# Four-layer AdaLN kernel on one core: modulation by rows, input in three pieces, a masked triangle, a 64-row last tile, and a new order in the last feed-forward's slot

## What is computed

```
mod = (silu(c) @ wmod).reshape(16, 6, 1, 256)     # per layer: sa, ca, ga, sb, cb, gb
ga  = (2*(ga >= 0) - 1) * max(|ga|, 0.25)          # gb the same
h = layernorm(x) * (1 + ca) + sa ; x = x + ga * attention(h)
h = layernorm(x) * (1 + cb) + sb ; x = x + gb * feed_forward(h)
```

## Time and profile before

| | us |
|---|---|
| median of three runs | 2000.65 |
| lowest, highest | 1992.62, 2005.60 |
| profiled execution, own time | 1990.36 |
| its span (first to last instruction) | 1987.9 |
| TensorE busy in the span | 1742.5 |
| VectorE busy | 1369.3 |
| GpSimd busy | 936.9 |
| ScalarE busy | 758.7 |

### The profile page before, as it was taken

How to read it: one execution, slowest core, us unless ns; L and a number is a source line. 1 busy time by engine, 2 the same in 40 slices (tenths; PEclk the granted TensorE clock), 3 DMA queues, 4 the chain that set the end, 5 groups by cost and what they waited for, 6 DMA issues and landing times.

```text
span 1987.9 us, 41551 instructions
## 1 busy us (share of the span) xinstructions
PE 1742.5 (88%) x14264; PEld 1252.0 (63%) x14264; DVE 1369.3 (69%) x3592; ACT 758.7 (38%) x1530; POOL 936.9 (47%) x984
## 2 busy tenths in 40 slices
PE   8999999689997999999999878889867788998776
PEld 5666665589994555555555556666656566886443
DVE  5788888365554566666666658888746776886765
ACT  3555554122221656565656531111122213443332
POOL 1467666575554446464545353223243223664333
PEclk7999998799997999999999989999998888999887
DMA  6100000100006564545455300000001000000111
GB/s 219 49 18 11 16 16 7 33 10 11 8 14 116 130 118 83 117 88 114 90 110 94 69 13 11 8 8 8 22 26 41 15 15 14 17 13 14 40 34 48
DMA packets 70565, 93.86 MB, mean 47 GB/s; under 512 B 10408, under 2 KB 64792, under 8 KB 67224
## 3 DMA queue, kind: packets, MB, share of 16 engines
q1 hardware_dynamic: 70440, 92.15, 20.6%
HBM read 61.84 MB, written 29.49 MB: 46 GB/s over the span
## 4 chain that ended last, share of the span: by engine, by line
PE 59%; DVE 19%; issue 8%; POOL 7%; ACT 5%; DMA 1%; DVEq 1%; SPq 0%; ACTq 0%; POOLq 0%
PE PS L1101 17%; PE PS L2093 4%; POOL l_ms L1063 3%; DVE negmax L2421 3%; PE PS L2183 3%; PE PS L2057 3%; PE PS L1268 3%; PE PS L529 2%; ACT pw L2336 2%; PE PS L2118 2%; PE PS L2077 2%; DVE xn L519 1%; PE PS L1813 1%; PE PS L2196 1%; PE PS L790 1%
## 5 line engine op out<-in xcount | busy, mean ns | idle before, releaser
L2421 DVE TENSOR_REDUCE negmax<-PS 128x2 f32<-128x512 f32 (+1 forms) x384 | 246.9, 685 | 167.6 <-PE PS L2093 161.7
L560 POOL TENSOR_TENSOR X<-X,y_sb 128x512 f32 (+1 forms) x128 | 164.1, 1282 | 121.7 <-DVE y_sb L555 116.7
L539 ACT ACTIVATE hT<-PS,modT 128x256 f32<-128x256 f32 x256 | 130.5, 562 | 139.8 <-PE PS L529 138.2
L1101 PE MATMUL PS<-we_hi,h_parts 128*128 128x512 f32 x512 | 177.6, 407 | 1.7 <-POOL h_parts L1550 1.5
L555 DVE TENSOR_TENSOR y_sb<-PS,ga_sb 128x512 f32<-128x512 f32 x96 | 66.2, 689 | 156.8 <-PE PS L1101 50.3
L2336 ACT ACTIVATE pw<-PS 128x512 f32<-128x512 f32 x256 | 139.2, 600 | 73.2 <-PE PS L2093 73.2
L519 DVE TENSOR_SCALAR xn<-X,mv,rs 128x256 f32 (+1 forms) x256 | 153.4, 640 | 5.7 <-POOL rs L512 4.1
L1101 PE MATMUL PS<-l_h_parts,lut_hi 128*128 128x256 f32 (+1 forms) x768 | 144.8, 290 | 6.7 <-POOL l_h_parts L1234 6.7
L510 POOL TENSOR_TENSOR rs<-mv,eps 128x2 f32<-128x2 f32 x128 | 26.8, 209 | 259.4 <-DVE mv L503 259.2
L1101 PEld LDWEIGHTS PS<-l_h_parts,lut_hi 128*128 128x128 f32 (+1 forms) x768 | 117.1, 183 | 9.7 <-issue 5.4
L1644 DVE SCALAR_TENSOR_TENSOR l_acc<-PS,rt_g,l_acc 128x256 f32<-128x256 f32 x256 | 105.8, 475 | 21.2 <-PE PS L1101 21.0
(11 more groups left out here) (294 smaller groups left out, 4412.0 us busy)
## 6 DMA issues: line engine op xcount, KB each, us to landing
ga_sb<-ga_dram SPq DMA_DIRECT2D x128, 128.0 KB, 2.9
qk_dram<-qk_parts SPq DMA_DIRECT2D x64, 192.0 KB, 2.8
KS<-qk_dram SPq DMA_DIRECT2D x32, 384.0 KB, 6.1
QS<-qk_dram SPq DMA_DIRECT2D x32, 384.0 KB, 9.2
qk_dram<-qk_parts SPq DMA_DIRECT2D x64, 128.0 KB, 2.8
wmod<-in_wmod SPq DMA_DIRECT2D x4, 1536.0 KB, 13.5
qk_dram<-qk_parts SPq DMA_DIRECT2D x64, 64.0 KB, 2.5
y_out<-X SPq DMA_DIRECT2D x16, 256.0 KB, 2.2
```

The costliest lines, as they stand in the source:

```text
L539: last_ = act.activation(hT[b.par][:, kh, :], PS[:, 0, kh * T:(kh + 1) * T], ACT.Identity, bias=modT[:, sub, 0, kh, bass.ds(b.n, 1)], scal ...
L560: pool.tensor_tensor(xb(b), xb(b), y_sb[b.par][:, :, :], ALU.add).then_inc(s.x.sem, 1)
L1101: last_ = pe.matmul(out, x.bitcast(F32R), y.bitcast(F32R), start=start and n == 0, stop=stop and n == 2)
L2421: dve.tensor_reduce(to, src, AX.X, ALU.max, negate=True).then_inc(s.max.sem, 1)
```

## The change

Six edits.

1. **Modulation by rows.** TensorE now makes shifts and scales as rows too: per half of the contraction three matmuls of 16 x 512 that write to partitions 0, 64 and 96 of one PSUM bank. ScalarE copies two of the three blocks to `mod_row`, and eight transposes of 16 rows give the columns. ScalarE's exponentials come after the copy of layer 0.
2. **Input in three pieces.** Batches 0 and 1 come behind the second wmod, batches 2 and 3 ahead of the weights of L0_attn, the rest as before.
3. **Decay masked in its triangle.** The mask is multiplied into the first 128 of 256 columns of each head alone, and this is done after layer 2's modulation instead of layer 0's. The wait for all gates moves from the start of L0_attn's TensorE program to behind the first product.
4. **64-row last tile.** The inner width is cut in 4 x 128 + 112 + 64. For the last tile gate and up lie side by side in the weights, so one product with 128 outputs makes both. The low half of that tile is made by VectorE, which puts it in the free 64 partitions beside the high half; the down product of the tile takes two matmuls instead of three.
5. **Fills spread evenly** over slots 0 to 3 of L0_ffn, and KS filled as float32 words with two bfloat16 ones each.
6. **New order of L3_ffn's slot** on TensorE, ScalarE and VectorE.

```diff
+            def rows(i):
                 w = wmod[i][:, :, :].rearrange("p k (s d) -> p k s d", s=SECTIONS)
                 pe.wait_ge(wmod_in[i], 16)
+                if i >= 2:
+                    pe.wait_ge(M["ga"], i - 1)
+                    pe.wait_ge(M["row"], i - 1)
                 for kh in range(KH):
-                    last_ = pe.matmul(PS[0:B, 1 + i, :], scT[:, i, kh, :], w[:, kh, 2:SECTIONS:3, :],
-                                      start=kh == 0, stop=kh == KH - 1)
+                    for r, of in ((0, slice(2, SECTIONS, 3)), (64, slice(0, 2)), (96, slice(3, 5))):
+                        last_ = pe.matmul(PS[r:r + B, ROW_BANK[i], :], scT[:, i, kh, :], w[:, kh, of, :],
+                                          start=kh == 0, stop=kh == KH - 1)
                 last_.then_inc(M["rows_ps"], 1)
...
+            def columns(i):
+                pe.wait_ge(M["row"], i + 1)
+                if i >= 2:
+                    pe.wait_ge(M["col"], i - 1)
+                for c in range(2):
+                    for m in range(KH):
+                        for sub in range(2):
+                            at, r = (c * KH + m) * B, 64 + 32 * sub
+                            last_ = pe.transpose(PS[:, 3 + 2 * (i % 2) + sub, at:at + B], mod_row[i % 2][r:r + B, c, m * P:(m + 1) * P],
+                                                 ident[r:r + B, r:r + B])
                 last_.then_inc(M["col_ps"], 1)
...
+            rows(0)
+            columns(0)
+            rows(1)
+            early(ln_transpose, pe)
+            for i in range(2, LAYERS):
+                rows(i)
+                columns(i - 1)
+            columns(LAYERS - 1)
...
+            def row(i):
+                act.wait_ge(M["rows_ps"], i + 1)
+                if i >= 2:
+                    act.wait_ge(M["col_ps"], i - 1)
+                for r in (64, 96):
+                    last_ = act.activation(mod_row[i % 2][r:r + B, :, :].rearrange("p c d -> p (c d)"), PS[r:r + B, ROW_BANK[i], :], ACT.Copy)
+                last_.then_inc(M["row"], 1)
+
+            for i in range(LAYERS):
+                row(i)
+                if i == 0 and first == 0:
+                    l0a_tables(act)
+                if i == 1 and first == 0:
+                    act.wait_ge(M["col"], 1)
+                    early(modulate, act)
...
-                    if first == 0:
-                        dve.wait_ge(setup["exp"], 1)
-                        dve.tensor_tensor(l0_decay[:, :, :], l0_decay[:, :, :],
-                                          causal[:, :].unsqueeze(1).broadcast_to([P, HEADS, T]), ALU.mult).then_inc(setup["decay"], 1)
+                if i == 2 and first == 0:
+                    dve.wait_ge(setup["exp"], 1)
+                    dve.tensor_tensor(l0_decay[:, :, 0:P], l0_decay[:, :, 0:P],
+                                      causal[:, 0:P].unsqueeze(1).broadcast_to([P, HEADS, P]), ALU.mult).then_inc(setup["decay"], 1)
...
+                        if m == FT - 1:
                             for kh in range(KH):
+                                last_ = matmul3(pe, PS[:, 1 + m % 3, 0:T], [x[:, kh, INTER - TAIL:INTER + TAIL] for x in both_w],
                                                 [l0_h_parts[i.par][:, c, kh, :] for c in range(2)], kh == 0, kh == 1)
...
+                        for n, w in ((P, down_w[0]), (TAIL, down_w[1])):
+                            last_ = pe.matmul(bank(4)[:, t * D:(t + 1) * D], hid_parts[b.par][0:n, 0, FT - 1, t * P:(t + 1) * P].bitcast(F32R),
+                                              w[0:n, FT - 1, :].bitcast(F32R), start=False, stop=n == TAIL)
...
+                        if m == FT - 1:
+                            dve.wait_ge(*s.hid_hi(i, FT))
+                            dve.wait_ge(*s.hid_lo(i, FT - 1))
+                            dve.tensor_tensor(hid_parts[i.par][TAIL:P, 0, m, :].bitcast(F32R), hid[m % 3][0:r, :],
+                                              hid_parts[i.par][0:r, 0, m, :], ALU.subtract).then_inc(s.hid_lo.sem, 1)
...
             def slot(i):
+                if i.ok:
+                    products(i)
+                if (i - 2).ok:
+                    wide_gates_T(i - 2)
                 if (i - 1).ok:
                     rows_T(i - 1)
-                if (i - 2).ok:
-                    wide_gates_T(i - 2)
-                if i.ok:
-                    products(i)
-                    tokens(i)
                 ahead(ln_transpose, pe, pl, i, 1)
-                if i.ok:
-                    norms(i)
                 if (i - 2).ok:
                     out(i - 2)
+                if i.ok:
+                    norms(i)
+                    tokens(i)
```

```diff
             if n < 2:
-                pool.memset(QS[n][:, :, :].bitcast(F32), 0.0).then_inc(setup["a_zero"], 1)
...
+                pool.memset(QS[n][:, :, :].bitcast(F32), 0.0)
+                pool.memset(l1_vpad[n][:, :, :, :], 0.0).then_inc(setup["a_zero"], 1)
             else:
...
+                pool.memset(KS[n - 2][:, :, :].bitcast(F32), TWO_ONES)
+                pool.memset(mparts[n - 2][:, :, :].bitcast(F32), 0.0).then_inc(setup["a_zero"], 1)
```

More of the change, by code:

```diff
@@ L164, in layout @@
     age = age[:, 0:P]
[L166 to L169, removed]
+    tail = np.arange(INTER - TAIL, INTER)
+    order = np.concatenate([np.arange((FT - 1) * P) % INTER, tail, tail])
+    down = np.ascontiguousarray(a["L0_ffn_down_idx"].T)[order].reshape(FT, P, D).transpose(1, 0, 2)
+    up = a["L0_ffn_up_idx"].T
+    both = two(np.concatenate([a["L0_ffn_gate_idx"].T, up[:, INTER - TAIL:], up[:, 0:INTER - TAIL]], 1))
+    out["l0_idx"] = np.concatenate([both.reshape(P, -1), down.reshape(P, -1)], 1)
     out["l0_lut"] = a["L0_ffn_lut"]
@@ L277, in build @@
         out_done = sem("out_done")
-        mod_sems = {n: sem("mod_" + n) for n in ("silu", "rows_ps", "col_ps", "col", "sign", "clip", "both", "ga")}
+        mod_sems = {n: sem("mod_" + n) for n in ("silu", "rows_ps", "row", "col_ps", "col", "sign", "clip", "both", "ga")}
         X = sb("X", [P, B, TT, D])
@@ L489, in ln_stats @@
             if pl == 0:
-                if b.reg is None and b.off < 4:
+                if b.reg is None and b.off < 2:
                     dve.wait_ge(x_in[0], 16)
+                elif b.reg is None and b.off < 4:
+                    dve.wait_ge(w_in[0], 16 * len(weights[0]))
                 else:
@@ L619, in mod_tensor @@
                 last_.then_inc(M["rows_ps"], 1)
[L620 to L628, removed]
@@ L1144, in slot @@
                     for t in range(TT):
-                        for m in range(FT):
+                        for m in range(FT - 1):
                             r = rows_of(m)
@@ L1877, in slot @@
                     act.activation(l3_mx[i.par][:, :], p[0:NS + E, T:2 * T], ACT.Identity, bias=l3_c0[:, 0:1]).then_inc(s.mx.sem, 1)
[L1878 to L1881 removed]
+                if (i - 1).ok:
+                    route_exp(act, pl, s, i - 1)
+                ahead(modulate, act, pl, i, 1)
+                if i.ok:
                     act.wait_ge(*s.s_ps(i))
@@ L1886, in slot @@
                                    scale=l3_roww[:, 0:1]).then_inc(s.z.sem, 1)
-                ahead(modulate, act, pl, i, 1)
+                    act.wait_ge(*s.hfree(i))
+                    if (i - 2).ok:
+                        act.wait_ge(*s.y1(i - 2))
+                    act.activation(l3_ht[i.par][:, :, :].rearrange("p t d -> p (t d)"), bank(2), ACT.Copy).then_inc(s.ht.sem, 1)
             slots(act, slot, -1, (4, 14), B)
@@ L1947, in slot @@
             def slot(i):
-                if (i - 1).ok:
-                    ratio(i - 1)
                 ahead(ln_apply, dve, pl, i, 1)
+                ahead(ln_stats, dve, pl, i, 2)
                 if (i - 2).ok:
@@ L1957, in slot @@
                 if (i - 1).ok:
-                    choice(i - 1)
+                    ratio(i - 1)
                 if (i - 2).ok:
@@ L1966, in slot @@
                                                  bank(4)[:, t * D:(t + 1) * D], ALU.mult, ALU.add).then_inc(s.y1.sem, 1)
-                ahead(ln_stats, dve, pl, i, 2)
+                if (i - 1).ok:
+                    choice(i - 1)
             slots(dve, slot, -2, (4, 14), B + 1)
@@ L2689, in build @@
         tables = [(l0_ld[:, :], rows(ins["l0_ld"])), (l0_age[:, :], ins["l0_age"]), (causal[:, :], ins["causal"])]
-        weights = {0: [(l0_w[n][:, :, :], ins["l0_w" + n]) for n in "qkvo"] + [
+        weights = {0: [(X[:, 2:4], ins["x"][2:4].rearrange("b t p d -> p b t d"))] + [(l0_w[n][:, :, :], ins["l0_w" + n]) for n in "qkvo"] + [
             (l0_wg1[:, :, :], ins["l0_wg1"]), (l0_wg2[:, :], ins["l0_wg2"]), (rank[:, :, :], ins["rank"]),
```

73 lines of the change are left out of this document (33 added, 40 removed).

## The result

| | before | after |
|---|---|---|
| median of four runs, us | 1997.77 | 1937.5 |
| lowest, highest | 1992.62, 2005.60 | 1935.13, 1940.81 |
| profiled execution, own time | 1990.36 | 1938.25 |
| its span | 1987.9 | 1936.1 |

The changed kernel takes 0.9696 [0.9658, 0.9734] of the time before. The sum of the prediction, 53 us, was made against the profiled execution; the two profiled executions differ by 52.1. The medians differ by 60.3, because the profiled execution of before lay 7 under its median and that of after did not.

A forecast was written before the change was run, and what follows sets the result against it. TensorE was taken to bound L0_ffn and the setup, a dependence loop L3_ffn; 6.5 + 19.7 + 27 = 53 us gave 1937 from the profiled execution, 1948 from the median, so 1944 was forecast, range 1924 to 1972.

The forecast's parts named there:

- the cases that I had set apart: Column groups in series 0.08, VectorE held more 0.08 or less 0.04, L3_ffn's order does nothing 0.05, slower 0.03.
- The loop of L3_ffn: In L3_ffn the next batch's modulation stands behind y1, closing a dependence loop of 10.2 us, the slot.
- The slot of 7.85: L3_ffn's new slot: VectorE full, two small operations held 0.5 and 1.1 us beside GpSimd's pair (1.27 and 1.26 us).
- the 6.4 given: L3_ffn's slot in us if GpSimd's pair holds no VectorE operation; time 1928, chance 0.04.
- 27 us: Gain forecast for L3_ffn: 2.4 us a slot over 11 full steps, range 16 to 35.
- At either TensorE clock: L3_ffn's slot is 7.85 us whether TensorE's first products go at 1.2 GHz or faster; the PE loop at 1.2 is 7.65.
- over 90% busy: Sign expected in L3_ffn: VectorE busy over 90% of a slot, with 7.9 us from add to add.
- Setup, 6.5: Setup ahead of L0_attn: k starts at 36.7 to 40 instead of 44.61, gain 4.6 to 8, taken 6.5 us.
- TensorE's walk: Setup: rows 3.5 us a layer, transposes up to 1.7, columns 3 at 31.5, TensorE done 10 us earlier.
- The 1 to 3 us for stretched operations: Setup: the mask and two gate steps on VectorE may each be stretched once beside GpSimd, 1 to 3 us.
- L0_ffn's tail, 14.2: L0_ffn's last tile: eight matmuls fewer, 0.95 us a slot over 15 slots, gain 14.2 us (14 to 15).
- L0_ffn's fills, 5.5: L0_ffn: spreading GpSimd's fills removes a 6.7 us stall and costs 1.2 over four slots, gain 5.5 (4.5 to 6.7).

The follow-up runs named there:

- l3_scalar_tensor: Changed kernel with L3_ffn's ScalarE and TensorE in the new order, VectorE as before: 1974.8 us, L3_ffn 167.8.
- l3_scalar_alone: Changed kernel with only ScalarE in the new order of L3_ffn, TensorE and VectorE as before: 1936.7 us, L3_ffn 135.7.
- fills_old: Changed kernel with the fills for L1_attn in old order and size, two of 3.51 us in L0_ffn's third slot: 1949.7 us, L0_ffn 235.1.
- l1_split_early: Changed kernel with GpSimd's two splits of q and k for L1_attn's first batch one place earlier in L0_ffn's last slot: 1941.9 us.

## Why the prediction was right

The time was 1937.5 for 1944 and the sum 52.1 for 53, and the cases that I had set apart did not occur. That the sum came within 1 us is in part luck: the parts that I counted gave 57.2 (9.5 + 19.5 + 28.2), and L1_attn, which I had not counted, was 5.4 longer. Within L0_ffn one part was 1.1 under and the other 0.8 over. Step by step:

*The loop of L3_ffn* (modulation behind y1): right, and shown, since ScalarE's order alone opens it. It missed that the first products would leave the half clock (1.03 us for 1.98). It also did not see that TensorE's new order costs 32 us without VectorE's (l3_scalar_tensor against l3_scalar_alone: 167.8 and 135.7), so that VectorE's edit is there to make good TensorE's.

*The slot of 7.85*: right in size (mean 7.85) and in mechanism. Two operations are held beside the pair; in the slot shown they cost 0.77 and 0.85 us, where I had 0.5 and 1.1. With the pair gone the slot is 6.25, near the 6.4 given. 27 us was 28.2. "At either TensorE clock" held in part: at a granted clock of 1.00 the full slots took 7.6 to 7.9 us, at 0.8 they took 8.0 to 8.4 in this trace and 7.8 to 7.9 in fills_old's. VectorE is not "over 90% busy", though: 6.64 of 7.59 us, with 0.6 of wait for TensorE's `out`. It is a loop through `out` and y1 more than a full engine.

*Setup, 6.5*: it was 9.1 to 9.5, beyond my 8. Mis-sized was TensorE's walk: the transposes took 0.4 to 0.6 us, not 1.7, and the rows of layer 3 took 1.90 and not 3.5. So VectorE began the mask at 27.5, where I had 30.4. The 1 to 3 us for stretched operations were about right. The mask was not stretched (2.27), but two gate steps took 0.88 and 1.65 us for 0.41 and 0.68, and `set_wo` 1.36 for the 0.60 of before: 2.2 together. It ended at 35.9, where I had 36.7 before the margin. k's start gives 8.5 of the gain. The input in three pieces was not taken out alone.

*L0_ffn's tail, 14.2*: 13.1 (248.2 to fills_old's 235.1; the tail was not taken out alone). The ordinary slot fell by 0.88 to 0.94, where 0.95 was worked out, and the slot under the fill, where TensorE was not the bound, not at all; the first stretch, counted at nothing, gave 1.2.

*L0_ffn's fills, 5.5*: 6.3. The cost left in slots 1 to 3 (14.1, 13.3 and 13.6 for 13.05) is 1.8 us and not 1.2. But the stall that is gone had grown: beside slots of 13.05, one of 20.7 costs 7.6 us and not 6.7.

*Not foreseen*: L1_attn's 5.4 us. The entry's part could have been read, as l1_split_early shows: the tail tile of the last slot comes after GpSimd's splits, so the chain to KS and QS starts only as much earlier as the rest of L0_ffn does.

*The median*: the forecast lay between 1937 (profiled execution) and 1948 (median); the changed kernel's own runs centre on the first.

## What to carry to other kernels

Undo a reordering engine by engine: here one engine's order held the whole gain, and a second one lost 32 us until a third was changed with it. Small VectorE steps that stand beside GpSimd's large ones are worth an operand in PSUM, or work that isn't held ahead of them. A loop worked out from durations at the half clock can be too long once the engine waits less. Compare phases, not whole times, where the clock of one long phase moves the time by more than the edit.

## What the runs showed of the hardware

Three column groups of 16 columns ran at no extra time (12 matmuls in 3.61 us, 4 in 3.57), in whichever order they were written. A VectorE step of 16 elements took 1.02 us beside a GpSimd operation with both operands in SBUF and 0.18 with one in PSUM. With the same instructions L1_attn's TensorE busy time lay between 519 and 532 us, at granted clocks of 0.97 to 0.94. The same four products took 1.98 us at a granted clock of 0.50 and 1.03 at 1.00.
